# Tile 1's first norm and transposes inside tile 0's recurrence, out-projection pieces in another place of the attention loop, and tile 0's expert norm block by block

## The reference, cut to what matters

```python
# x: (8, 4096, 1024) f32; one row of the batch per core
x = x + mixer(layernorm(x))      # xp = silu(x W_in); alpha, beta = sigmoid(xp W + b); v = tanh(xp W + b)
                                 # h_t = alpha_t h_(t-1) + beta_t v_t over all 4096 tokens
                                 # out = (h silu(h)) W_out
x = x + ffn(layernorm(x))
# ffn(z):
h = rmsnorm(z); q = h Wq + bq; k, v = split((h Wdown + bdown) Wup + bup)   # 16 heads of 64
att = softmax(q k^T / 8) among the 16 heads of one token; out = att v
z = z + (out Wo + bo)
h2 = rmsnorm(z); gate = softmax(h2 Wg + bg)                                 # 8 experts
return z + sum_e gate_e (h2 We_e)
```

## Time and profile before

| | us |
|---|---|
| three runs, median (lowest, highest) | 2241.36 (2018.11, 2354.70) |
| the profiled execution | 2015.93 |
| span of its slowest core, core 3 (whose trace is read) | 2014.3 |
| spans of the other cores | 2005.1 to 2014.2 (core 0: 2014.2) |
| PE busy | 1896.7, 94% of the span |
| DVE, ACT, POOL busy | 1267.4, 739.4, 211.6 |

### The profile page before, as it was taken

How to read it: one execution, slowest core, us unless ns; L and a number is a source line. 1 busy time by engine, 2 the same in 40 slices (tenths; PEclk the granted TensorE clock), 3 DMA queues, 4 the chain that set the end, 5 groups by cost and what they waited for, 6 DMA issues and landing times.

```text
span 2014.3 us, 32221 instructions; the slowest of 8 cores (2005.1 to 2014.3 us)
## 1 busy us (share of the span) xinstructions
PE 1896.7 (94%) x11008; PEld 900.6 (45%) x11008; DVE 1267.4 (63%) x2146; ACT 739.4 (37%) x1971; POOL 211.6 (11%) x208
## 2 busy tenths in 40 slices
PE   4787667999999999999999999999999999999899
PEld 2343333444444444454444544444444544444444
DVE  2745657865478646776468755786467764676544
ACT  3343634431435333533325334343335424352200
POOL 3621120210001100020001200021000200011000
PEclk9888868999999999999999999999999999999999
DMA  8995373657534283335642375333843364423343
GB/s 266 341 324 137 69 136 65 175 149 223 196 126 147 105 257 140 147 127 157 220 168 108 126 204 204 114 142 123 249 150 133 126 179 158 145 105 126 126 149 144
DMA packets 72909, 326.48 MB, mean 162 GB/s; under 512 B 31136, under 2 KB 31136, under 8 KB 39712
## 3 DMA queue, kind: packets, MB, share of 16 engines
q1 hardware_dynamic: 67520, 277.75, 40.8%
q0 software_dynamic: 5232, 46.68, 9.2%
HBM read 303.97 MB, written 48.23 MB: 175 GB/s over the span
## 4 chain that ended last, share of the span: by engine, by line
PE 88%; DVE 4%; issue 3%; DMA 2%; ACT 2%; POOL 1%; DVEq 0%; SPq 0%; ACTq 0%; POOLq 0%
PE bank L369 43%; PE bank L429 14%; PE bank L456 6%; PE bank L604 5%; PE bank L506 5%; PE bank L411 5%; PE bank L542 2%; DMA we<-wall 2%; PE bank L585 2%; PE bank L574 1%; PE bank L527 1%; PE bank L477 1%; DVE F L919 1%; PE bank L571 1%; PE bank L490 1%
## 5 line engine op out<-in xcount | busy, mean ns | idle before, releaser
L369 PE MATMUL bank<-we,h2T 128*128 128x512 bf16 x4096 | 938.5, 380 | 7.6 <-DVE gat L1105 6.5
L887 DVE SCALAR_TENSOR_TENSOR xs<-bank,gat,xs 128x512 f32<-128x512 f32 x512 | 384.1, 750 | 393.9 <-PE bank L369 393.0
L369 PEld LDWEIGHTS bank<-we,h2T 128*128 128x128 bf16 x4096 | 386.4, 98 | 432.8 <-issue 18.5
L297 POOL TENSOR_TENSOR F<-F,sml 128x512 bf16<-128x512 bf16 x128 | 132.9, 1038 | 1445.7 <-DVE sml L1014 1445.7
L429 PE MATMUL bank<-F,wm 128*128 128x512 bf16 x1280 | 280.2, 381 | 4.8 <-POOL wm L285 4.0
L795 ACT ACTIVATE F<-bank,sml 128x128 bf16<-128x128 f32 x512 | 182.0, 371 | 220.0 <-DVE sml L1006 220.0
L429 PEld LDWEIGHTS bank<-F,wm 128*128 128x128 bf16 x1280 | 125.7, 98 | 158.2 <-issue 9.1
L927 DVE SCALAR_TENSOR_TENSOR R<-R 128x512 f32<-128x512 f32 x64 | 46.0, 718 | 102.1 <-ACT R L721 102.0
L815 ACT ACTIVATE tm<-R,sml 128x1024 bf16<-128x1024 f32 x32 | 36.9, 1152 | 193.7 <-DVE R L1065 193.7
L795 ACT ACTIVATION_READ_ACCUMULATOR F<-bank,sml 128x1 f32 x512 | 107.2, 209 | 0.0
L715 ACT ACTIVATE R<-bank,cpfs 128x512 f32<-128x512 f32 x64 | 44.0, 688 | 163.0 <-DVE F L919 115.6
(11 more groups left out here) (118 smaller groups left out, 1852.5 us busy)
## 6 DMA issues: line engine op xcount, KB each, us to landing
we<-wscr SPq DMA_DIRECT2D x128, 1024.0 KB, 5.9
wm<-wscr SPq DMA_DIRECT2D x84, 1024.0 KB, 5.0
wscr<-wall POOLq DMA_DIRECT2D x16, 1024.0 KB, 10.2
out<-xs SPq DMA_DIRECT2D x32, 512.0 KB, 5.1
xs<-wall POOLq DMA_DIRECT2D x14, 1024.0 KB, 9.3
we<-wall POOLq DMA_DIRECT2D x14, 1024.0 KB, 12.1
xs<-x SPq DMA_DIRECT2D x7, 2048.0 KB, 9.0
wscr<-wm SPq DMA_DIRECT2D x6, 1024.0 KB, 18.2
```

The costliest lines, as they stand in the source:

```text
L297: gp.tensor_tensor(pb[j % 3][:, :].rearrange("p (g n) -> p g n", n=128), pb[j % 3][:, :].rearrange("p (g n) -> p g n", n=128), sml[:, RS + ...
L369: mm = pe.matmul(b[:, :], hT[:, kc * 512 + tb * 128:kc * 512 + (tb + 1) * 128], we[ui % NE][:, kc * 512:(kc + 1) * 512], start=(kc == 0), ...
L887: v.scalar_tensor_tensor(dst, bk[6 + k % 2][:, :], gat[(t - 1) % 2][:, tb * 8 + e:tb * 8 + e + 1], dst, OP.mult, OP.add).then_inc(v_ec, 1)
```

## The change

Four things are moved; the arithmetic is the same.

1. Tile 1's x is loaded once block 2 of tile 0's x has landed. DVE takes its statistics ahead of the gate loop `abv(0)`, ACT computes the reciprocal deviation inside `win(0)`, behind the Silu of chunk 4, and applies the norm to two blocks behind `win(0)` and two at chunk 1 of `abv(0)`. PE does the 32 transposes of t1(1) in two halves behind pieces 8 and 14 of `abv(0)`, in banks 6 and 7; DVE copies them out in chunks 2 and 4. win(1) follows `abv(0)` directly and uses banks 6 and 7.
2. In `abv(1)`, DVE empties t2(0) in chunks 4 and 6 (before 5 and 6), PE does the second part of t2(0) behind piece 20 (before 17) and wdn(0) behind piece 23 (before 20); ACT's `zev(0)` moves to match.
3. In the rounds 0 to 7 of att(0), PE does a piece of wout(1) behind the transposes instead of ahead of them, and DVE empties it a round later, ahead of its copy of the transposes.
4. Tile 0's expert norm goes block by block (`ln3_first`): for each block Square, Ln, Exp, then the apply of the block before it, written to `F1`; DVE's `nb3_first` follows in the `wo(0)` loop and, for block 3, ahead of `xu(0)`.

```diff
 # sp_prog
-        sync.wait_ge(c_cm, 2)
+        sync.wait_ge(s_xb[2], 16)
         load_x(1)
 # pe_prog
+        def t1(t, parts):
+            for p in parts:
                 if p == 0:
                     pe.wait_ge(a_l1a, t * 4 + 4)
-                    if t == 1:
-                        pe.wait_ge(a_abv, 21)
-                if p == 3 and t == 1:
-                    pe.wait_ge(a_abv, 22)
+                if t == 1 and p >= 2:
+                    pe.wait_ge(v_t1, 3 + p)
+                bb = bkb[6 + p % 2 if t == 1 else p]
...
         def win(t):
...
-                if t == 1 and mc == 0:
-                    pe.wait_ge(a_abv, 24)
...
+                    if t == 1 and mc == 0 and kc == 0:
+                        pe.wait_ge(v_t1, 8)
...
-                    mm = pe.matmul(bk[4 + mc % 2][:, :],
+                    mm = pe.matmul(bk[(6 if t == 1 else 4) + mc % 2][:, :],
...
         def abv(t):
...
+                if t == 0:
+                    if ci == 8:
+                        t1(1, (0, 1))
+                    if ci == 14:
+                        t1(1, (2, 3))
                 if t == 1:
                     if ci == 14:
                         t2(0, (0, 1))
-                    if ci == 17:
+                    if ci == 20:
                         t2(0, (2, 3))
-                    if ci == 20:
+                    if ci == 23:
                         wdn(0)
...
         def att(t):
...
                 if t >= 1:
                     ec(t, 1)
-                elif j < 8:
-                    wout(1, j)
...
                 mm.then_inc(p_ptv, 1)
                 if t >= 1:
                     ec(t, 1)
+                elif j < 8:
+                    wout(1, j)
                 pe.wait_ge(v_ptv, t * 16 + j + 1)
 # act_prog
         def win(t):
...
+                if t == 0 and mc == 4:
                     load_set(SET_LNE)
                     ln1_rstd(1)
                     load_set(SET_SILU)
+            if t == 0:
+                ln1_app(1, 0)
+                ln1_app(1, 1)
...
+                if t == 0 and mc == 1:
+                    ln1_app(1, 2)
+                    ln1_app(1, 3)
-                if t == 1 and mc == 7:
+                if t == 1 and mc == 8:
                     zev(0)
...
+        def ln3_first():
+            n2 = N2[0]
+            for b in range(NB + 1):
+                if b < NB:
+                    s.wait_ge(v_u, 2 * b + 2)
+                    s.activation(out=tm1[:, b * D:(b + 1) * D], in_=ub[:, b * D:(b + 1) * D], func=AF.Square,
+                                 bias=sml[:, n2 + b:n2 + b + 1], accum_out=sml[:, SS + b:SS + b + 1])
+                    s.drain()
...
+                if b >= 1:
+                    s.wait_ge(v_nb3, b)
+                    s.activation(out=F1[:, (b - 1) * D:b * D], in_=ub[:, (b - 1) * D:b * D], func=AF.Identity,
+                                 scale=sml[:, RU + b - 1:RU + b],
+                                 bias=sml[:, NB3 + b - 1:NB3 + b]).then_inc(a_h2, 1)
 # dve_prog
         def abv(t):
...
-                if t == 1 and mc in (5, 6):
-                    t2(0, range(4 * (mc - 5), 4 * (mc - 4)))
+                if t == 0 and mc in (2, 4):
+                    t1(1, range(mc - 2, mc))
+                if t == 1 and mc in (4, 6):
+                    t2(0, range(2 * mc - 8, 2 * mc - 4))
...
         def att(t):
...
-                if t == 0 and j < 8:
-                    x1ev(1, j)
                 if j + 1 < 16:
                     rsum(t, j + 1)
+                if t == 0 and 1 <= j <= 8:
+                    x1ev(1, j - 1)
...
         def wo(t):
...
+                if t == 0 and u in (2, 4, 6):
+                    nb3_first(u // 2 - 1)
```

More of the change, by code:

```diff
@@ L632, in pe_prog @@
         pe.wait_ge(s_c1, 48)
-        t1(0)
+        t1(0, range(4))
         win(0)
         abv(0)
-        t1(1)
         win(1)
@@ L854, in act_prog @@
         att(0)
-        ln3(0)
+        ln3_first()
         zev(1)
@@ L1116, in dve_prog @@
         ln1_nm(0)
-        t1(0)
+        t1(0, range(4))
+        for u in range(8):
+            ln1_bn(1, u)
+        ln1_aggr(1)
+        ln1_nm(1)
         v.wait_ge(g_set, 1)
         abv(0)
-        t1(1)
         gmul(0, NCH - 1)
```

56 lines of the change are left out of this document (25 added, 31 removed).

## The result

The changed kernel takes 1983.53 us (four runs, 1982.96 to 1983.88). The kernel before, run beside it, takes 2018.11 and 2018.66. The ratio is 0.9827 (95% interval 0.9803 to 0.9851): 1.7% faster, clear of no change. The forecast was 1980 in a range of 1968 to 1990, called no change within 2%. The time lies 3.5 us above the forecast; the call, no change that can be measured, was wrong. Executions in which the cores of a die ran at a lower clock and the time was over 1.5% longer are left out of all times and ratios, and where this happened more mildly in a profiled execution (casts 1 to 3 late; qm and km on their own queue) the spans are given for cores 4 to 7 alone.

What follows compares the result with a forecast made beforehand. TensorE was taken as the bound from 340 us on, unchanged; the gain was how much earlier expert matmuls start. 2.5 + 17.9 + 12 + 2.9 = 35.3 us off 2015.93 gave 1980.6, say 1980, range 1968 to 1990.

Steps and rivals of the forecast that it cites:

- Part 1: Front, up to tile 0's `wout(0)`: x lands at 40 us, all cores meet at about 120 us; 2.5 us saved.
- Part 2: Tile 1's gate loop: earlier emptying of transposes ends PE's waits for DVE, so `kv(0)` starts 17.9 us earlier.
- My list of signs: Closing checks; for tile 1's gate loop: no wait over 1 us, `wq(0)` 65 us behind `wout(0)` (before 75.6).
- Part 3: First half of tile 0's attention: rounds fall from 5.86 to 4.1 us; 12 us saved, bounds 5.5 to 15.9.
- Part 4: Tile 0's expert norm: DVE's first copy comes 8.1 us behind the last sum, before 11.0; 2.9 us saved.
- The clock of transposes: Transposes put between gate matmuls: 16 priced at 0.9 us; by the skill's rule some 2.5 us more, sum 1983.
- Full clock and an early x: Rival: attention bound by DVE at 3.6 us a round, x at 35 us; 1973 (1967 to 1977), chance 0.27.
- The slower one: Rival at the front: x load starved behind POOL's weight loads while ACT and PE wait; above 2020, chance 0.02.

## Why the prediction was right and wrong

**The call: the step that failed is its bound.** The text says "2% of it is 40 us, about what a measurement of this kernel can tell from no change". Of the forecast saving, 35.3 us or 1.75%, it says "as no change by that bound though it is a gain". The four runs of the changed kernel lie within 0.92 us, the two of before within 0.55, and the interval is 0.25% to either side, 5 us. In the later experiments 15 and 16 executions of the kernel before spread over 8.4 and 10.6 us, up to 0.5%. The saving is seven times that. The chip was not misjudged in this call; the forecast time itself, held against this interval, says faster. I had seen three times before with a median of 2241.36 and a lowest of 2018.11, called the profiled execution the one to compare with, and yet kept a bound that fits neither the spread of such executions nor the size of the effect.

**The sum.** 2018.4 less 1983.5 is 34.9 us against 35.3 forecast. Part of this is luck: the forecast started from the profiled execution, 2015.93, and against it the profiled execution of the changed kernel, 1982.96, gains 33.0; the mean span gains 32.0. And it did not come by its terms:

- *Part 1, forecast 2.5, measured 5.8 on the mean* (6.5 on core 0, 8.0 on core 3). For the slowest core I had 7 and it was 8.0: the last cast ends at 88.33 on core 3, where I took 89.1, and DVE's multiply there ends 0.8 us earlier than before, not 1.5 later; the chunks after it do take 4.67, but the stretch to `wout(0)` gains 7.2 where I had 8.5. The mis-sized step is "A lead won before the casts end comes from earlier weights, and the new wait for x takes it away: all cores now meet at about 120 us". They don't meet: 111.2 to 119.0, nearly the old spread. There was no wait for x to take anything. It landed at 30.9 us, not 40:

```profile
xs<-x SPq DMA_DIRECT2D x1, 2048.0 KB, 16.0
```

  16.0 us from issue to landing (14.3 to 17.4 over the eight cores) where I had taken some 24, from the 26.2 beside the same competition. Issued at 14.88, it stands ahead of POOL's weight loads (15.37), whose packets begin at 21 us only. The queues of core 0 in 12 to 20 us after, and in the same stretch before:

```profile
q1 hardware_dynamic: 528, 2.00, 77.4%
```

```profile
q0 software_dynamic: 209, 1.58, 56.4%
q1 hardware_dynamic: 218, 0.76, 27.7%
```

  The cost of it fell elsewhere: the second half of the first weight unit is cast at 27.95 us instead of 19.64, PE waits 2.77 for it and then runs the first 32 matmuls of `win(0)` in 9.86 us (before 7.90). The granted clock reads 1.00 in both stretches, so that no row says why they are slower. So the gate loop starts at 49.05 on core 0, near the forecast 51.5 but for another reason. The runs with the late x show what a real wait for x costs: 14.34 us at PE on core 0, and 4 to 6 us in the end where km is not waited for.

- *Part 2, forecast 17.9, measured 17.9 and then cut by half.* DVE's first keys start at 178.59, 62.33 us behind `wout(0)`; before it was 80.24 on core 3 (207.25 less 127.01), which makes 17.9. Core by core the gain is 17.7 to 18.7. Step by step: second transposes 51.0 us behind `wout(0)` and without a wait, 0.44 at `wdn(0)` (forecast 0.5), `wq(0)` after 59.4. My list of signs says 65 there, which is a slip: it sets the 185.7 us of the text, worked out from `wout(0)` at 127.0, against the new 120; the text's own figure is 58.7. The step that failed is the last sentence of the part, "the qm and km loads move with the event they wait for", by which the wait for km was put at nothing. Their *issue* does, to the microsecond. Their landing depends on what is ahead of them in SP's queue and on the casts, one of which moves with the same event and the other with a place that moved less. The prediction looked at the event that lets the loads go, and not at the bytes in the queue at that time. The queue runs show it: with the gap between the casts put back, or with a queue of its own for qm and km, the wait is gone on all eight cores. It costs 9.0 us ahead of the scores by the means (10.9 with the 1.9 that the stage would have gained).

- *Part 3, forecast 12, measured 14.9 in the changed kernel and 16.1 to 16.4 when undone.* "I take 4.1" a round is the mis-sized step; a round takes 3.59. The rival with full clock had this at 3.6 and DVE as the bound, and it is what happened: all pieces but the first at 1.89, granted clock 0.90 in the stretch (the earlier trace rows had 0.75), DVE busy for 21.32 of 30.60. The forecast for eight rounds was 33 us; from the first piece at 215.57 to the end of the eighth product at 244.83 it is 29.3, where the kernel before took 46.9 on core 3 and 47.9 on core 0 (227.25 to 275.13). Of the 18.6 on core 0, 1.6 are given back ahead of the first piece (5.2 us behind the first score, before 3.6) and 1.9 in the second half, 15.1 stay. For these two I had 0.9 and 1.4.

- *Part 4, forecast 2.9, measured 3.4 in the stage and 2.0 to 3.3 in the time when undone.* DVE's rows go as worked out: the small products wait 0.59 and 0.65 for ACT, the last one 2.07 (forecast 1.9), then `xu(0)` 4.87, and the first copy follows at once. The last sum ends at 290.30 and the copy starts at 297.42, 7.1 us later; the forecast's 8.1 held 1.0 of lateness in the loop beside the same 7.1. The 2.0 us come from one profiled execution each, in which the rest is 0.7 and the attention 0.5 longer with the norm by blocks; over all executions it is 3.3.

- *The clock of transposes.* I priced them at 0.9 behind matmuls. The trace agrees: 16 transposes in 1.06 us, 66 ns each, at 167.23 in the rows above. By the rule of the Trainium skill, TensorE: Matmul & The Clock Gate, Part 4: PE-mode transpose, that the full clock does not engage for them, they would have taken what they took behind a wait of 7 us, 1.86; the rows differ from it, and the granted clock reads 1.00 at 167.23. That the rule's sum of 1983 is the measured time is chance.

**The rivals.** "Full clock and an early x", 1973 with 0.27, had both effects right. The attention was bound by DVE at 3.6 us a round, and x came early, though not by even turns: it had the engines to itself at first. Its 1973 would have been about the time but for the wait for km: with that wait removed and nothing else changed in the four parts the time is 1974.5 (only casts 2 and 3 late). No rival named the wait. The slower one looked at the x load behind POOL's weight loads, the right kind of mechanism (a load starved behind another queue) at the wrong load.

## What to carry to other kernels

When a change moves the place at which a load is issued, ask what will be in its queue and on the other queues at that new time; "it moves with its event" holds for the issue alone. Where two streams are tied to places that move by different amounts, the gaps between them are part of the design, and a shorter stage can close one. And hold a forecast against the spread of executions of this kernel (here at most 0.5% among 16 of them, and 0.25% as the interval of the ratio), not against a bound taken for all kernels: 1.7% is a gain.

## What the runs showed of the hardware

The DMAs that cast from DRAM to DRAM move here in packets of 33 KB that take 4.5 us each (192 to 199 us of the changed kernel, core 0), and SP's queue then moves one packet of 4 KB for each of them: 17 to 18. It moves 0.07 MB in these 7 us and 1.15 MB in 8 us without a cast. The engines aren't full in the sense of bytes then (94 GB/s in these 7 us, 143 in the 8 without a cast), so that neither the share of busy engines nor the bandwidth in the page shows that a queue is starved; the number of packets by queue does.

With tile 1's x issued 0.5 us ahead of POOL's weight loads, the first packet of POOL's queue moves about 4 us behind its issue on four cores (1, 2, 5, 7) and 6 to 7 us behind it on the others. So x goes alone until 21 us on core 0, and lands there in 16.0 us instead of 24.0 (core 3: 17.4 instead of 26.2). Before the change, with no x in SP's queue, that first packet came 1 to 3 us behind the issue; on core 0, with loads issued at 14.22, POOL's queue had moved 1.58 MB by 20 us. What takes the time, no run here tells.
